# Value weights loaded from ScalarE's queue, and the last pair's last group given a place of its own

## The reference

```
q, k, v = layernorm(x) @ Wq, ctx @ Wk, ctx @ Wv          # 16 heads of 64
o = softmax(q k^T / 8) v                                 # over 77 keys
x = x + tanh(g_xattn) * (o @ Wo + bo)
idx = argmax(log_softmax(logits) - log(-log(u)))         # one of 8 weights
out = x + tanh(g_ffn) * (layernorm(x) @ W[idx] + b[idx])
```

## Time and profile before

| | |
|---|---|
| three runs | 1049.84, 1053.71, 1053.37 us; median 1053.37 |
| the profiled execution's own time | 1052.05 us |
| its span | 1050.3 us |
| TensorE busy | 1035.0 us of the span |
| VectorE, ScalarE, GpSimd busy | 851.7, 744.7, 438.8 us |
| TensorE's granted clock | 0.998 of full speed over the span |

### The profile page before, as it was taken

How to read it: one execution, slowest core, us unless ns; L and a number is a source line. 1 busy time by engine, 2 the same in 40 slices (tenths; PEclk the granted TensorE clock), 3 DMA queues, 4 the chain that set the end, 5 groups by cost and what they waited for, 6 DMA issues and landing times.

```text
span 1050.3 us, 21821 instructions
## 1 busy us (share of the span) xinstructions
PE 1035.0 (99%) x6065; PEld 588.1 (56%) x6065; DVE 851.7 (81%) x1800; ACT 744.7 (71%) x2712; POOL 438.8 (42%) x635
## 2 busy tenths in 40 slices
PE   9998899999999999999999999999999999999998
PEld 7634455555555555555555555555555555555555
DVE  4877988888888887888888887888888887888876
ACT  3578887766776677767776677767776676767762
POOL 0575344444433343444433443444433443444322
PEclk9999999999999999999999999999999999999999
DMA  8414466655666656655666656655666656655656
GB/s 312 104 26 107 95 128 133 137 115 117 127 136 135 135 128 134 136 119 110 131 137 135 135 123 139 136 115 110 132 138 137 136 121 135 135 114 113 132 115 141
DMA packets 383639, 135.02 MB, mean 129 GB/s; under 512 B 361728, under 2 KB 363316, under 8 KB 383540
## 3 DMA queue, kind: packets, MB, share of 16 engines
q1 hardware_dynamic: 383476, 134.09, 59.0%
q0 software_dynamic: 64, 0.00, 0.0%
HBM read 27.48 MB, written 16.78 MB: 42 GB/s over the span
## 4 chain that ended last, share of the span: by engine, by line
PE 92%; DVE 4%; ACT 2%; DMA 1%; SPq 1%; issue 1%; POOL 0%; DVEq 0%
PE banks L1356 83%; PE banks L1580 3%; PE banks L1459 1%; PE banks L1386 1%; PE banks L1395 1%; PE banks L1467 1%; ACT work L858 1%; DMA work<-work 1%; DVE vw_area L1062 1%; ACT vw_area L811 1%; PE banks L1448 1%; DVE work L1162 1%; DVE work L425 0%; DMA fold_area<-in_ctx 0%; DVE fold_area L1070 0%
## 5 line engine op out<-in xcount | busy, mean ns | idle before, releaser
L858 ACT ACTIVATE work<-banks,red,cst 128x77 f32<-128x77 f32 x1024 | 410.4, 431 | 89.1 <-DVE red L1153 89.1
L1356 PE MATMUL banks<-fold_area,work 128*128 128x462 f16 (+1 forms) x2304 | 410.6, 336 | 1.4 <-DMA work<-work 0.7
L1356 PE MATMUL banks<-vw_area,work 128*128 128x512 f16 x1674 | 373.1, 380 | 2.6 <-DMA work<-work 2.6
L1356 PEld LDWEIGHTS banks<-fold_area,work 128*128 128x128 f16 x2304 | 223.9, 97 | 176.2 <-DMA work<-work 1.2
L1356 PEld LDWEIGHTS banks<-vw_area,work 128*128 128x128 f16 x1674 | 164.1, 98 | 188.5 <-DMA work<-work 2.9
L425 DVE SCALAR_TENSOR_TENSOR work<-work 128x256 f16<-128x256 f32 (+3 forms) x444 | 240.1, 575 | 3.5 <-ACT work L881 3.0
L858 ACT ACTIVATION_READ_ACCUMULATOR work<-banks,red,cst 128x1 f32 x1024 | 225.7, 220 | 0.0
L1151 DVE TENSOR_REDUCE stats<-banks 128x6 f32<-128x462 f32 (+1 forms) x192 | 112.1, 584 | 109.2 <-PE banks L1356 108.7
L1356 PE MATMUL banks<-work 128*128 128x256 f16 x1302 | 162.4, 272 | 1.6 <-DVE work L1237 1.6
L1356 PEld LDWEIGHTS banks<-work 128*128 128x128 f16 x1302 | 126.7, 98 | 33.4 <-issue 1.3
L703 POOL TENSOR_TENSOR stats<-stats,cst 128x1 f32<-128x1 f32 x64 | 12.5, 196 | 284.7 <-DVE stats L1187 284.7
(11 more groups left out here) (145 smaller groups left out, 814.6 us busy)
## 6 DMA issues: line engine op xcount, KB each, us to landing
work<-in_x SPq DMA_DIRECT2D x64, 256.0 KB, 2.8
out<-work SPq DMA_DIRECT2D x63, 256.0 KB, 2.2
work<-work SPq DMA_TRANSPOSE x254, 3.0
fold_area<-in_L_xattn_Wo SPq DMA_DIRECT2D x4, 512.0 KB, 8.9
work<-in_L_ffn_W SPq DMA_DIRECT2D x2, 1024.0 KB, 6.9
fold_area<-in_L_xattn_Wq SPq DMA_DIRECT2D x2, 1024.0 KB, 12.3
fold_area<-in_L_xattn_Wk SPq DMA_DIRECT2D x2, 768.0 KB, 12.0
fold_area<-in_L_xattn_Wv SPq DMA_DIRECT2D x2, 384.0 KB, 6.2
```

Of the source, the lines that this page charges most:

```text
L858: nc.scalar.activation(probs_of(h, h + 1), s_bank(m, k)[:, (h - h0) * J:(h - h0 + 1) * J], ACT.Exp, bias=nmx[:, h:h + 1], scale=exp_scale, ...
L1356: mm = nc.tensor.matmul(ps, lhs(l), rhs(r), start=first and n == 0, stop=last and n == 2, skip_group_check=onto)
```

## The change

Three edits. ScalarE issues the three loads of Wv, ahead of all its other work, and SyncE no longer does. Group 3 of the last pair alone is staged in a new place, `last_group`, and its turn counts on a semaphore of its own, `last_turned`; ScalarE no longer waits for the turn of group 2 there, and makes its high half ahead of tile 62's. And VectorE's order in `last_steps` is another.

```diff
+        last_group = c.take(HD).bitcast(F16).rearrange("p (s n) -> p s n", s=2)
...
-        def group_stage(g):
+        def group_stage(g, last=False):
+            if last:
+                return last_group
...
         def _(sp):
             for b in range(B):
                 sp.dma_start(ctx_raw[:, b, :], ctx_in[b, :, :]).then_inc(ctx_loaded[b], 16)
-            for n, (h0, h1) in enumerate(V_PIECES):
-                cols = slice(h0 * P, h1 * P)
-                sp.dma_start(wv_raw[:, :, cols], wv.rearrange("(k p) n -> p k n", p=P)[:, :, cols]).then_inc(wv_loaded[n], 16)
...
-                        turn_group(3)
+                        turn_group(3, is_tile(o, m, NT))
...
         def _(act):
 
+            for n, (h0, h1) in enumerate(V_PIECES):
+                cols = slice(h0 * P, h1 * P)
+                act.dma_start(wv_raw[:, :, cols], wv.rearrange("(k p) n -> p k n", p=P)[:, :, cols]).then_inc(wv_loaded[n], 16)
...
-                if positive(o, m, 2) or g > 0:
+                last = g == 3 and is_tile(o, m, NT - 4)
+                if (positive(o, m, 2) or g > 0) and not last:
                     act.wait_ge(x2T_turned, nth_pair(o, m, 16 * GROUPS) + 16 * g)
...
                     if is_tile(o, m, NT):
                         corner_high()
+                    group_high_of(*pair, 3 if m % 2 == 0 else 1)
+                    if is_tile(o, m, NT):
                         lone_high(NT - 2)
-                    group_high_of(*pair, 3 if m % 2 == 0 else 1)
...
                 lone_low(NT - 2)
+                group_low_of(*pair, 3)
                 for i in (0, 1, 3):
                     added(*pair, i)
-                group_low_of(*pair, 3)
                 attention_sum(*last)
                 dve.wait_ge(x2_stats, NT)
                 x2_variance(*last)
+                added(*pair, 2)
                 x2_normalized(*last)
-                added(*pair, 2)
                 lone_low(NT - 1)
+                added(*pair, 4)
                 lone_output(NT - 2, 0)
                 lone_output(NT - 2, 1)
-                for i in range(4, PRODUCTS):
-                    added(*pair, i)
+                added(*pair, 5)
+                added(*pair, 6)
                 lone_output(NT - 1, 0)
                 lone_output(NT - 1, 1)
...
                 if i == 4:
-                    pe.wait_ge(x2T_turned, nth_pair(o, m, 16 * GROUPS) + 64)
+                    if ends:
+                        pe.wait_ge(last_turned, 16)
+                    else:
+                        pe.wait_ge(x2T_turned, nth_pair(o, m, 16 * GROUPS) + 64)
```

More of the change, by code:

```diff
@@ L240, in flamingo_layer @@
         x2T_high, x2T_low = ([sem(f"{w}{n}") for n in range(2)] for w in ("x2T_high", "x2T_low"))
+        last_turned = sem("last_turned")
         corner_loaded, corner_hi, corner_lo = sem("corner_loaded"), sem("corner_hi"), sem("corner_lo")
@@ L472, in load_x, with turn_group @@
                 sp.dma_start(xr[:, ml, :], x[batch, rows, :]).then_inc(x_loaded[ml], 16)
-            def turn_group(g):
+            def turn_group(g, last=False):
                 sp.dma_start_transpose(group_place(g).rearrange("p s j k n -> p (s j k) n"),
-                                       group_stage(g).rearrange("p s n -> p (s n)")).then_inc(x2T_turned, 16)
+                                       group_stage(g, last).rearrange("p s n -> p (s n)")).then_inc(last_turned if last else x2T_turned, 16)
             sp.wait_ge(pads_set, 1)
@@ L876, in probs_high, with group_high @@
                                      scale=2.0 ** PROB_BITS).then_inc(p_hi, 1)
-            def group_high(g, value):
-                nc.scalar.activation(group_stage(g)[:, 0, :], value, ACT.Copy, scale=2.0 ** XN_BITS).then_inc(x2_hi, 1)
+            def group_high(g, value, last=False):
+                nc.scalar.activation(group_stage(g, last)[:, 0, :], value, ACT.Copy, scale=2.0 ** XN_BITS).then_inc(x2_hi, 1)
             def group_high_of(o, m, g):
-                if positive(o, m, 2) or g > 0:
+                last = g == 3 and is_tile(o, m, NT - 4)
+                if (positive(o, m, 2) or g > 0) and not last:
                     act.wait_ge(x2T_turned, nth_pair(o, m, 16 * GROUPS) + 16 * g)
@@ L899, in group_high_of @@
                 else:
-                    group_high(3, room_c)
+                    group_high(3, room_c, last)
             def lone_high(n):
@@ L1196, in x2_normalized, with group_low @@
                 nc.vector.tensor_scalar(room_b if m % 2 else room_a, xr[:, m, :], mv2[:, 0:1], rstd2, ALU.subtract, ALU.mult).then_inc(x2n_ready, 1)
-            def group_low(g, value):
-                low(group_stage(g)[:, 1, :], value, 2.0 ** XN_BITS, group_stage(g)[:, 0, :]).then_inc(x2_lo, 1)
+            def group_low(g, value, last=False):
+                stage = group_stage(g, last)
+                low(stage[:, 1, :], value, 2.0 ** XN_BITS, stage[:, 0, :]).then_inc(x2_lo, 1)
             def group_low_of(o, m, g):
                 dve.wait_ge(x2_hi, nth_pair(o, m, GROUPS) + g + 1)
-                group_low(g, (room_a, room_b, room_a, room_c)[g])
+                group_low(g, (room_a, room_b, room_a, room_c)[g], g == 3 and is_tile(o, m, NT - 4))
             def lone_low(n):
```

## The result

The changed kernel took 1057.64 us in the median of 8 runs (1055.46 to 1058.83); the kernel before, run beside it, 1051.76 us (1049.84 to 1054.59, 8 runs). The ratio is 1.0049, with a 95% interval of 1.0035 to 1.0062: slower by 5.2 us (5.9 between the medians), where 0.2 us faster had been forecast, and above the stated range, which ended at 1055.5. The profiled execution of the changed kernel took 1055.46 us, with a span of 1053.7; before, 1052.05 and 1050.3.

The account below looks back on a forecast made before the run. TensorE, busy 1035.0 of 1050.3 us, was taken as the bound. Head +0.4 and tail -0.58 gave -0.2 us: 1051.9 against the profiled execution, 1052.5 from the median of four runs; range 1050.0 to 1055.5.

Parts of the forecast that it names:

- Wv's loads on ScalarE, +0.4 us: Head: issue time moves at no cost, but Wv's data beside the context's delays the chain's start by 0.4 us.
- rival 1: Head: Wv delays the context, TensorE starts 1.1 to 3.8 us later; 1053.3 to 1055.9 us; 30%.
- because of that room: Head, fifth microsecond: DMA engines only 0.32 busy at 82 GB/s, the reason for taking +0.4 us, near the low end.
- Wv's larger packets: Head: if these win over equal turns between queues, the context's delay grows from 1.15 up to 3.8 us.
- The bound, 3.8 us at worst: Head: all of Wv, 1.57 MB at 410 GB/s, goes ahead of the context, delaying it 3.8 us at most.
- rival 4: Head: context over 1.5 us late, TensorE's clock falls, the 13.22 us projection takes twice as long; 1067 us; 2%.
- granted in full in every slice: Whole kernel: TensorE's clock read at its upper level throughout, the argument against a clock fall.
- no stretch shows one: Whole kernel: the trace before was said to hold no clock fall after idling, such as the skill's page describes.
- The tail, -0.58 us: Tail: L1180 starts as soon as tile 63's attention ends, so its whole chain and `lone(63)` come 0.58 us earlier.
- The 1.4 us that Wv's first piece had to spare: Head, before: Wv's first piece lands at 7.9 us, the projection takes it at 9.31, so Wv is not waited for.
- SyncE's shorter row, nothing: Head: without 1.47 us of Wv's issue, SyncE's later loads go out 1.5 us earlier, off the chain; worth nothing.
- The measure: Baseline: profiled execution 1052.05 us, three runs' median 1053.37, 3.9 apart; median of all four 1052.7, from which it predicted.

Follow-up runs that it names:

- E3: The changed kernel with issuers swapped: ScalarE issues the context's loads, SyncE Wv's and then its others; 1056.85 us, ratio 1.0049.
- E4: The changed kernel with ScalarE waiting for the whole context to land before issuing Wv's loads; 1058.7 us, ratio 1.0065.
- E5: The changed kernel with only Wv's first piece on ScalarE, the other two back in SyncE's queue behind the context; 1051.28 us, ratio 1.0005.
- E6: The changed kernel with GpSimd's two loads of the gates issued only when the context has landed; 1054.51 us, ratio 1.0023.
- E7: The changed kernel with 14 and 36 more identity multiplications ahead of the third and fourth batch's transposes; 1054.09 us, ratio 1.0021.
- E2: The kernel before with the tail's edits alone, Wv's loads staying with SyncE; 1052.25 us, ratio 1.0004.
- E1: The kernel before with only Wv's three loads moved to ScalarE, old tail kept; 1057.7 us, ratio 1.0055.
- E10: E5 (first piece of Wv on ScalarE, tail's edits) with the gates' loads held back until the context has landed; 1049.35 us, ratio 0.9967.
- E8: The changed kernel with ScalarE waiting for GpSimd's memset, so Wv's loads are issued from 3.14 us on; 1054.96 us, ratio 1.0027.
- E9: E2 (tail's edits, Wv with SyncE) with the gates' loads held back until the context has landed; 1052.23 us, ratio 0.9995.

## Why the prediction was wrong, point by point

*Wv's loads on ScalarE, +0.4 us.* This step failed. It was +4.2 in the profile, the context's last batch landing at 11.22 instead of 6.47. I had its mechanism as rival 1, with 30%, and took the sum's value from the other end, "because of that room" in the fifth microsecond: DMA engines 0.32 busy. That row told how busy the engines were with what one queue gave them, not what share the context would keep beside a second queue. In the changed kernel they were 0.99 busy from 3 to 4 us, and the context's queue got 14%. That swapping the issuers changes nothing (E3), that alone the context lands at 5.32 (E4), and that a quarter of the bytes does no harm (E5) shows that Wv's loads beside it were the cause, with the gates' loads (E6) making it worse.

The rule of the Trainium skill that I had set against the row ("DMA: Bandwidth & Descriptors", "Queues, rings and completion order": the engines take turns between queues, packet by packet) was the better guide: it foretold the delay. The size it does not explain. Nor do "Wv's larger packets", as I had it in rival 1: by the view's own count q10's are about 1.0 KB (0.29 MB in 290) and q1's 1.4 (0.05 MB in 37). Why the shares were 85% against 14% stays open.

*The bound, 3.8 us at worst.* Wrong too: the context landed 4.75 us later. The bound took the DMA engines to be full. They moved 136 and 94 GB/s when it counted, and the gates' small packets were part of that (E6).

*The clock, rival 4, 2%.* The condition (the context over 1.5 us late) and the mechanism came; the chance and the price were wrong. The granted clock did fall while TensorE waited 3.41 us. I had priced it at 13 us, as if the whole projection ran slow; keeping TensorE running gave back 2.9 us by the ratios of E7 and the changed kernel, 3.5 by their medians. And my reason against it was a misreading: "granted in full in every slice". The timeline of the kernel before has:

```profile
7.40 1.91 PE L1369 MATMUL banks<-work 128*128 128x128 f32 x8
9.10 5.14 PE L1386 MATMUL banks<-fold_area 128*128 128x308 f32 x16
```

The 8 multiplications of the identity took 1.91 us, where E7 has 1.04, and the projection 13.27 (9.10 to 22.37), where E7 has 12.44. TensorE was slow there, under a clock column that reads 1.00. Also, the mean of 0.998 was in my table, and "no stretch shows one" was false: the profile of before has a stretch at 0.50 from 120 to 123 us, right behind a wait of TensorE, which one digit of a slice hides. The first row is from the timeline, the second from stretches of 1 us, TensorE alone (its last three columns are clock, DMA share and GB/s):

```profile
119.97 7.68 PE L1356 MATMUL banks<-vw_area,work 128*128 128x512 f16 x27 [2.61 <-DMA work<-work]
120.00:121.00 1.00, 1.00 (x3) 0.50 0.96 373
```

In E2 the same 27 multiplications, behind a wait of 2.52 us, ran with the clock at 1.00 and took 6.00 us. So TensorE's clock can fall behind a wait of this length or not, and here it costs 1.7 us.

Together: with TensorE kept running, the changed kernel is 2.2 us above before (E7, 1.0021, tail's gain included); without, 5.2 (1.0049). The 2.9 us between are what the clock is worth, give or take 2 by the two intervals. They are not wholly an addition to before: in the two profiles the multiplications and the projection took the same (1.91 and 13.27, then 1.91 and 13.12), and the 3.4 us between their spans owe nothing to the clock.

*The tail, -0.58 us.* In the profile -0.68, by the steps foretold: L1186 0.04 us behind the attention, no wait ahead of product 4, 0.47 (0.5) ahead of product 6, 0.52 (0.4) ahead of `lone(63)`, L1202 2.63 us behind L1186 (2.6). But its worth was taken from one execution. E1's old tail lacks the stall, and E2 can't be told from before. The 1.4 us that Wv's first piece had to spare are of the same kind: in E2's profile, from the same queue, it landed at 9.11, and TensorE waited 0.97 us for it.

*SyncE's shorter row, nothing.* Right: u is there 0.9 us earlier (10.86) and nothing comes of it.

*The measure.* The forecast started from four runs of the kernel before, spread over 3.9 us. Of 78 more, those at a mean clock of 1.0 had a median of 1050.28 (22 runs), those at 0.998 of 1052.6 (36), and those at 0.997 of 1053.74 (15). A good part of that spread goes with the clock; the rest does not, for the 36 alone reach from 1050.44 to 1056.07.

## What to carry to other kernels

Before another engine's queue is put to use at the same time as the first load on the critical chain, count how much will then move beside the load that is waited for. But holding the second load back until the first has landed was no cure: E4 did so and was the slowest. One small piece in a second queue did no harm (E5), and with the gates held back it came with a gain (E10, 3.5 us); the whole weight was a loss. When a load becomes late and TensorE idles for it, add a price of the clock to that of the wait, taken from the duration of the same matmuls in fast and slow stretches.

A wait of half a microsecond seen in one profile may not be there in the next run. Compare the stall's cause (here the length of one DMA issue) in a second profile before counting on it.

## What the runs showed of the hardware that I had not expected

The granted clock of the profile can read 1.00 while TensorE runs slow: E8's projection took 15.47 us with 1.00 in every microsecond from 11 to 16, against 12.44 in E7. Its matmuls, all of one shape, took from 0.42 to 0.85 us each. The duration of the same matmuls was the surer sign. Timeline of E8:

```profile
11.32 15.63 PE L1395 MATMUL banks<-fold_area 128*128 128x308 f32 x48 [1.84 <-DMA fold_area<-in_L_xattn_Wv]
```

Two loads of 128 rows of 4 bytes held up large ones: with them issued later (E6), the eighth and ninth microsecond moved 326 and 334 GB/s instead of 136 and 94, and in E9, all in one queue, Wv's first piece landed 4.8 us after its issue instead of 5.5 (6.7 in E2). And a load just issued from a queue of its own may not move for almost 4 us (E8); why stays open.
